# Gathering rows of x for the first two pairs of each loop before the projected tables are stored

## What is computed

```
h = max(layernorm(x), 0);  xl = h@Wl+bl;  xr = h@Wr+br
m = leaky_relu(xl[src] + xr[dst] + w1*We);  logits = m@att
alpha = softmax of logits over the edges of one dst
x1 = x + batchnorm(gelu(h + sum(xl[src]*alpha) + bias))
h1 = max(layernorm(x1), 0)
e = relu(layernorm([h1[src], h1[dst]] @ msg_w + msg_b)) * w
messages = sum(e over dst) / count
out = x1 + gate*relu(layernorm([h1, messages]@upd_w + upd_b)) + (1-gate)*h1
```

## Time and profile before

| | us |
|---|---|
| median of 3 runs | 2380.59 (2380.45 to 2383.5) |
| the profiled execution | 2381.25 |
| its span in the trace | 2379.4 |
| busy: POOL, PE, DVE, ACT | 1612.2, 1634.4, 1535.0, 1021.9 |

### The profile page before, as it was taken

The page is one execution under the profiler, slowest core; times in us unless marked ns, Lnnn a source line. Parts: engine busy times, 40 slices in busy tenths (PEclk is TensorE's granted clock), DMA queues, the critical chain, the costliest instruction groups (busy, mean ns, idle before and its releaser), DMA issues.

```text
span 2379.4 us, 44459 instructions
## 1 busy us (share of the span) xinstructions
PE 1634.4 (69%) x9871; PEld 1205.1 (51%) x9934; DVE 1535.0 (65%) x4997; ACT 1021.9 (43%) x3829; POOL 1612.2 (68%) x1685
## 2 busy tenths in 40 slices
PE   5377787777777777878477776666766666666653
PEld 4255555555555555555365554444544445445542
DVE  7455656656656555655668766667666666666658
ACT  5143444443434443434443544444444434444337
POOL 1577777777777777777017777777777777777740
PEclk9699889888989999889677888888888888888786
DMA  8544444444444444443433434434344343343432
GB/s 229 145 87 94 93 87 95 89 91 94 91 91 94 86 95 93 88 94 76 130 116 72 102 88 94 92 86 93 85 94 92 86 94 84 94 92 88 92 91 68
DMA packets 208000, 228.63 MB, mean 96 GB/s; under 512 B 103119, under 2 KB 153700, under 8 KB 207877
## 3 DMA queue, kind: packets, MB, share of 16 engines
q0 software_dynamic: 54224, 112.59, 24.1%
q1 hardware_dynamic: 153046, 114.71, 17.4%
q10 hardware_dynamic: 672, 0.69, 0.1%
HBM read 194.60 MB, written 33.24 MB: 96 GB/s over the span
## 4 chain that ended last, share of the span: by engine, by line
POOL 51%; issue 19%; PE 12%; DMA 7%; DVE 6%; ACT 2%; POOLq 1%; SPq 1%; DVEq 0%; ACTq 0%
POOL room L692 51%; DMA room<-src_table,rec 6%; PE psum L800 2%; PE psum L861 2%; PE psum L782 1%; PE psum L725 1%; PE psum L772 1%; PE psum L866 1%; PE psum L767 1%; DVE stats L1220 1%; PE psum L879 1%; PE psum L790 1%; DMA room<-state 1%; ACT node_h L969 1%; PE psum L895 0%
## 5 line engine op out<-in xcount | busy, mean ns | idle before, releaser
L692 POOL DMA_INDIRECT room<-src_table,rec x1664 | 1597.2, 960 | 638.5 <-issue 495.9
L861 PE MATMUL psum<-room,ident 128*128 128x384 f32 (+1 forms) x512 | 298.2, 671 | 352.4 <-DMA room<-src_table,rec 317.8
L1105 ACT ACTIVATE room<-psum 128x128 f32<-128x128 f32 x832 | 219.3, 274 | 562.4 <-DVE room L1604 562.2
L1421 DVE TENSOR_TENSOR room<-psum,room 128x384 f32<-128x384 f32 (+1 forms) x256 | 151.1, 590 | 401.8 <-ACT room L1037 267.3
L1037 ACT ACTIVATE room<-psum 128x384 f32<-128x384 f32 (+1 forms) x256 | 131.6, 514 | 548.7 <-PE psum L772 541.0
L1604 DVE TENSOR_TENSOR room<-psum,msg_g 128x384 f32<-128x384 f32 (+1 forms) x256 | 150.5, 588 | 303.9 <-PE psum L866 300.2
L861 PEld LDWEIGHTS psum<-room,ident 128*128 128x128 f32 x512 | 93.9, 229 | 376.0 <-issue 309.0
L866 PEld LDWEIGHTS psum<-room 125*128 125x128 bf16 x2496 | 201.1, 114 | 149.8 <-issue 129.0
L800 PE MATMUL psum<-room 128*125 128x128 f32 x1664 | 264.5, 301 | 16.8 <-ACT room L1055 11.4
L879 PE MATMUL psum<-room 128*125 128x128 f32 x1664 | 273.4, 309 | 1.8 <-ACT room L1117 1.8
L772 PE MATMUL psum<-ident,room 128*128 128x128 f32 x832 | 150.6, 298 | 148.4 <-DMA room<-src_table,rec 146.7
(11 more groups left out here) (181 smaller groups left out, 2142.2 us busy)
## 6 DMA issues: line engine op xcount, KB each, us to landing
room<-dst_perm SPq DMA_DIRECT2D x128, 406.2 KB
room<-src_table,rec POOLq DMA_INDIRECT x1664
room<-dst_table SPq DMA_DIRECT2D x128, 62.5 KB
src_table<-rows SPq DMA_DIRECT2D x24, 224.0 KB
dst_table<-rows SPq DMA_DIRECT2D x24, 224.0 KB
st_in<-state SPq DMA_DIRECT2D x64, 64.0 KB
state<-st_out SPq DMA_DIRECT2D x64, 64.0 KB
st_in<-state SPq DMA_DIRECT2D x64, 62.5 KB
```

The costliest lines, as they stand in the source:

```text
L692: pool.indirect_dma_start(out=xg[:, u, t * P:(t + 1) * P], out_offset=None, in_=src_table[n][:, :], in_offset=bass.IndirectOffsetOnAxis(ap ...
L861: nc.tensor.matmul(msg_bank[b][:, cols], ident[:, :], xg[:, u, t0 * P:t1 * P], start=True, stop=False, skip_group_check=True)
L1105: i = nc.scalar.activation(sq[:, j * P:(j + 1) * P], msg_bank[b][:, j * P:(j + 1) * P], ACT.Square, accum_out=var_e[:, c, j:j + 1])
```

## The change

Gathers of the first two pairs (`RAW = 2`) of each loop read rows of x itself (loop 1) or of x1 (loop 2, from a new array `x1_rows` that SP stores), so they need no table. The gathered rows are then normed (DVE statistics, ACT scale), transposed (PE), relu (ACT), projected (PE) and the bias added (DVE), in place in `xg`. For pair 0 this stands before loop 1 (`raw_first`) and inside the own phase of the middle; for pair 1 it stands inside slot 0 and the start of slot 1 of each loop (`raw_second`).

The opening is also in another order. The number row of the destinations is loaded first on ACT's queue, ahead of the four arrays of weights, and is turned into float by ACT (it was POOL); POOL permutes it (it was ACT) and stores records and permutation (it was SP); `chunk_spans` on DVE stands before the first bias add, not before the fourth; 14 arrays of weights that only the second half needs are loaded by POOL after loop 1 (they were loaded by SP in the opening), and DVE centres `msg_w` there. SP loads the destinations of the first two pairs behind the last table rows, not ahead of them.

```diff
+RAW = 2
+            gather_pair(0, gat, 0, 0)
...
+            gather_pair(0, gat, 1, 1)
...
+            tables_stored(0)
+            def first_slot(k, u, end):
+                if type(k) is not int or k >= RAW:
+                    gather_pair(0, gat, k, u)
+            all_pairs(pool, first_slot, last, 0)
+            for to, v in last_weights:
+                pool.dma_start(to, v).then_inc(s_wc, 16)
...
+            for g, (t0, t1) in enumerate(GROUPS):
+                sp.wait_ge(s_x1, g + 1)
+                for p0, p1 in NODE_ROWS:
+                    sp.dma_start(node_cols(x1_rows, p0, p1, t0, t1), node_x[p0:p1, t0:t1, :]).then_inc(s_x1_out, 16)
...
+        RAW_NORM, RAW_TURN, RAW_FEATURES, RAW_PROJECT, RAW_ROWS = (range(i, i + 2 * NB, 2) for i in (1, 3, 4, 5, 6))
...
+        def raw_second(pe, n, k, b, weights):
+            if type(k) is int and k == 0:
+                raw_turn(pe, n, 1, b)
+                if b > 0:
+                    raw_project(pe, n, 1, b - 1, weights)
+            if type(k) is int and k == 1 and b == 0:
+                raw_project(pe, n, 1, NB - 1, weights)
...
                 for b in range(NB):
                     if there(k, 0, end):
                         msg_message(k, u, b)
+                    raw_second(pe, 1, k, b, msg_wc)
                     lagged(msg_sums, k, u, b, 3, end)
...
+            act.wait_ge(s_padded, 1)
+            load_field(act, 1)
             for to, v in first_weights:
                 act.dma_start(to, v).then_inc(s_wa, 16)
-            act.wait_ge(s_padded, 1)
-            load_field(act, 1)
+            act.wait_ge(s_padrow, 3)
+            act.wait_ge(s_edges[1], 48)
+            nc.scalar.activation(dst_f[0:NCH + 1, :], raw[0:NCH + 1, 1, :], ACT.Copy).then_inc(s_dstf, 1)
...
+            def raw_norm(n, r, b):
+                act.wait_ge(s_norm_scale, raw_part(n, r) + 1)
+                for t in range(*BLK[b]):
+                    rows_t = xg[:, r, t * P:(t + 1) * P]
+                    i = nc.scalar.activation(rows_t, rows_t, ACT.Identity, bias=raw_nmr[:, r, t:t + 1], scale=raw_rstd[:, r, t:t + 1])
+                i.then_inc(s_norm, 1)
...
-            tables(1, msg_b, {})
+            tables(1, msg_b, {11: lambda: raw_scale(1, 0, msg)})
+            raw_scale(1, 1, msg)
```

More of the change, by code:

```diff
@@ L445, in _ @@
             sp.wait_ge(s_padded, 1)
[L446 removed]
+            for f in (0, 2, 3):
                 load_field(sp, f)
@@ L560, in first_records, with first_destinations @@
             def first_records(n, s):
-                for k in range(3):
+                for k in range(RAW if n == 0 else 0, 3):
                     load_rec(s, k, k)
+            def first_destinations(n, s):
                 firsts = []
@@ L664, in _, with gather_pair @@
             pool.wait_ge(s_padrow, 3)
-            n = NCH + 1
-            pool.wait_ge(s_edges[1], 48)
-            pool.tensor_copy(dst_f[0:n, :], raw[0:n, 1, :]).then_inc(s_dstf, 1)
+            def gather_pair(n, s, k, u):
+                pool.wait_ge(s.rec[u], turns(s, k, u, U, 16, last))
+                first_rows = type(k) is int and k < RAW
+                table = (a["x"], x1_rows)[n] if first_rows else src_table[n]
+                for b, (t0, t1) in enumerate(BLK):
+                    if type(k) is not int or k >= U:
+                        if n == 0:
+                            pool.wait_ge(s.sum, nth(k - U, b + 1))
+                        else:
+                            pool.wait_ge(s.m, nth(k - U, b + 1))
+                    settle(pool)
+                    for t in range(t0, t1):
+                        pool.indirect_dma_start(
+                            out=xg[:, u, t * P:(t + 1) * P], out_offset=None, in_=table[:, :],
+                            in_offset=bass.IndirectOffsetOnAxis(ap=rec[:, u, t:t + 1].bitcast(I32), axis=0),
+                        ).then_inc(s.xg[u][b], 16)
@@ new lines, in tables_stored @@
+            def tables_stored(n):
+                for u in range(3):
+                    pool.wait_ge(s_src_out[u], 32 * (n + 1) * SLOT_GROUPS[u])
+            last = 0
+            gather_pair(0, gat, 0, 0)
+            pool.wait_ge(s_dstf, 1)
+            settle(pool)
+            for c0, c1 in STORE_ROWS:
+                pool.dma_start(rec_rows[c0:c1, 1, :], dst_f[c0:c1, :]).then_inc(s_rec, 16)
+            pool.wait_ge(s_edges[0], 48)
+            settle(pool)
+            for c0, c1 in STORE_ROWS:
+                pool.dma_start(rec_rows[c0:c1, 0, :].bitcast(I32), raw[c0:c1, 0, :]).then_inc(s_rec, 16)
@@ L1346, in list_block @@
                 dve.drain().then_inc(s_blk3, 1)
-            tables(0, b_lr, {0: opening, 1: lambda: x_stats(3), 2: later_columns, 3: chunk_spans, 6: count_pairs,
-                             7: lambda: list_block(0)})
-            edge_row_parts()
-            rest_of_weights(0)
+            last = 0
+            tables(0, b_lr, {0: opening, 1: lambda: x_stats(2), 2: lambda: x_stats(3), 3: later_columns, 6: count_pairs,
+                             7: lambda: list_block(0), 9: edge_row_parts, 11: lambda: rest_of_weights(0)})
+            raw_scale(0, 0, gat)
             rest_of_weights(1)
@@ L1512, in batch_stats @@
                 i.then_inc(s_bnst, 1)
+            dve.wait_ge(s_wc, NWC * 16)
+            dve.tensor_reduce(wmean[:, 0:2], msg_w[:, :, :], AX_X, ALU.add)
+            link(dve.tensor_reduce(wmean[:, 2:3], msg_b[:, D:2 * D], AX_X, ALU.add))
+            link(dve.tensor_scalar(wmean[:, 0:3], wmean[:, 0:3], 1.0 / D, None, ALU.mult))
+            for h in range(2):
+                link(dve.tensor_scalar(msg_wc[:, h * D:(h + 1) * D], msg_w[:, h, :], wmean[:, h:h + 1], None, ALU.subtract))
+            link(dve.tensor_scalar(msg_b[:, D:2 * D], msg_b[:, D:2 * D], wmean[:, 2:3], None, ALU.subtract))
+            dve.drain().then_inc(s_centred, 1)
             done = 0
```

265 lines of the change are left out of this document (183 added, 82 removed).

## The result

The changed kernel takes 2398.22 us (median of 6 runs, 2391.51 to 2401.17), the kernel before 2380.88 (6 runs, 2379.04 to 2383.5): ratio 1.0068, 95% interval 1.0055 to 1.0082. It is slower by 17 us. The prediction was 2372 with a range to 2388. The profiled execution took 2400.21 us, with a span of 2398.4.

What follows compares the result with a forecast made beforehand. It took the starts of late gathers, gated by ring and records, to bound the kernel. From 2381.25 us: loop 1 -21, middle +1, loop 2 +11, together -9, giving 2372; range 2357 to 2388.

Steps and rivals of the forecast that it cites:

- What bounds the kernel: Both loops: a loop ends as late as its gathers were started, so starts of late gathers are compared, 16.3 us a pair.
- The opening: Before loop 1: last add at about 65, POOL starts pair 2 10 us earlier, PE starts loop 1 at 90 as now.
- I take the first add at 24.3: Opening, DVE's first bias add: moved from 19.96 to 24.3, chunk work covered by a 4.13 us wait and 2.02 us of statistics.
- From the first add to the end of the last: Opening's tables: 2.0 us statistics, 3.0 weights' remainder, 1 smaller piece added, 5.9 removed, 2 us stall; last add at about 65.
- Slot 0 of loop 1: First slot, blocks one after another: 23 us in place of 12.0; pair 4 gathered at 123, 21 us gained (10 to 28).
- Middle and own phase: Between the loops: 1 us lost to weights (0 to 3), own phase starting at 1247, 2.5 us more inside it (0 to 7).
- Loop 2: Slot 0 takes 29 us (27 to 34), slot 1 17; pair 5 gathered at 1337, 11 us lost (3 to 22).
- Clock in the own phase: PE between the loops: low clock kept, granted 0.53; 13 transposes and projections take 10 us, against 5 at full clock.
- The second table load: ACT's second function table: counted with 1.28 us; with the skill page's drain of 1.38 us the sum would be 2373.4.
- B: Rival: PE stays at the low clock, own phase 6.5 us more, loop 2 loses 22, loop 1 gains 12; 2392, chance 0.17.
- D: Rival: opening or pair 0's raw chain 7 us late, gain 14 against loss 12 and 1; 2380, chance 0.15.
- A: Rival: slots keep up and POOL runs on, both loops give their 26 gathers; at most 2311, put at 2340, chance 0.07.

Runs made afterwards that it cites:

- features_late: Changed kernel with checked loop counts, ScalarE's features(g) again behind deviations and norm_rows(g + 2) in opening and middle; ratio 1.0062.
- copy_late: Changed kernel with weights first, features late, chunk work at group 3, pair 1's record behind group 2's stores, ScalarE's destinations copy behind features(1); 2382.70 us.
- one_raw_loop1: copy_late with only pair 0 raw in loop 1 and no raw pairs in loop 2; 2356.44 us.
- stats_early: copy_late with pair 0's statistics and scale moved from behind the tables into them, at group 5; 2385.60 us.
- opening_again: copy_late with ScalarE's copy of the destinations back at the head of its work; 2389.21 us.
- weights_second: copy_late with the weights issued behind the destinations again; 2389.31 us.
- weights_features: Changed kernel with weights first and features late, destinations copy and chunk work left as in the change; 2390.28 us.
- the control: Changed kernel with two loop counts checked against their bounds when loaded, run on the slower chip; 3108.95 us, ratio 1.0079.

## Why the prediction was wrong, point by point

- **What bounds the kernel** held: the marks at which late gathers start carried every total in the table, and the loops behind them kept their pace.
- **The opening failed**, and with slot 0 it took the whole gain of loop 1. Pair 4 was to be gathered at 123 and came at 148.25: 18.7 of these 25 us stand at PE's start of loop 1 (108.67 against 90), 5 in slot 0, 2 between the sum and the gather. The failed step is "I take the first add at 24.3", which rested on the 4.13 us wait and 2.02 us of statistics as a cover. It measured 37.02. All three pieces were named in that step, the copy, the second table and the features ahead of the square root "that wait for weights which now come second", and none was followed to a time. The copy put the first square root from 9.26 to 16.35. The weights, issued 2.6 us later than before, landed at 26.08, 21.2 us after their issue instead of 9.0; the sum had given this place, with the copy and the table load, 4.3 us in all. The chunk work, taken as 5.9 us, was to be hidden by the wait ahead of the first add. The wait stood ahead of it instead, for the second square root; it came at 28.33, took 8.5 us and lay bare. In features_late it did not: it began at 20.5, and the first add still waited 4.34 us for PE behind it. By the runs the copy and the weights are worth 9 us each with all else restored, and the order of the features 5 to 8 behind them. With the opening restored the time is that of the kernel before (2382.70), so this step explains the loss, but not all of the distance to the forecast.
- **From the first add to the end of the last** I took 41 us; 44.9 were measured, and 42.7 in copy_late. From there to the start of loop 1: taken 25, measured 27 and 26. The stall of 2 us on ScalarE's part was 7.8 at group 4 in the changed kernel (the add at 57.79 waits for PE), 0.5 in copy_late. That PE starts at 90.00 with the opening restored, where I had it at 90, is in part luck: the first add came 3 us earlier than in the forecast, the rest took 3 longer.
- **Slot 0 of loop 1**: taken 23, measured 28.0 and in copy_late 27.4. I took 5.5 to 6.7 us a block; blocks 1 to 3 took 7.2 to 7.8. One link was missing: the transposes of block 2 of pair 1 wait for VectorE to have emptied their bank, 3.60 us in the row at 126.22. Slot 1 to its sum: taken 10, measured 9.6. So even with the opening restored the gain was 16 (copy_late), not 21.
- **Middle and own phase**: weights 1 us, measured none (they are centred at 1148.15, under the wait for the state). The own phase was to start 9.3 us later, and starts at 1254.78, 17.1 later, of which 5.3 to 6.5 come from loop 1: 11 to 12 where 9.3 were taken.
- **Loop 2** held: slot 0 taken 29 (27 to 34), measured 32.4; slot 1 taken 17, measured 15.4; the loss of middle and loop 2 taken as 12, measured 13.9 in the distance. In copy_late it was 17.9, in the other kernels with two raw pairs 14 to 17: where loop 1 ends earlier, the loss of loop 2 is not smaller.
- **Clock in the own phase.** I let it stay at the 1.2 GHz level, with a granted clock of 0.53 before. It did not. The stretch now:

```profile
core 0: us, PE busy (x) PEld busy (x) DVE busy (x) ACT busy (x) POOL busy (x), PEclk, DMA share, GB/s
1255.00:1285.00 30.00, 18.01 (x123) 16.16 (x123) 28.44 (x53) 9.54 (x29) 23.60 (x22) 0.89 0.19 49
```

Eight update matmuls take 1.12 us from 1262 on, behind the first transposes of raw rows, instead of 2.06. In one_raw_loop1, without raw work there, they take 2.06 again. It brought no time, since VectorE is busy for 28.44 of 30 us. The Trainium skill (TensorE: Matmul & The Clock Gate, Part 1) says that activity releases the throttle; this trace agrees, with 0.89 granted where 0.53 was.

- **The second table load.** The rows at 12.15 and 15.05 are each followed by their operation 1.30 us after their start. The Trainium skill (ScalarE: Activation LUTs, What ACT_TABLE_LOAD costs) counts a further drain of 1.38 us; no row here shows one.
- **The rivals.** B named a slower end (2392) by the low clock in the own phase; the time came near it, the mechanism did not. D, an opening "7 us late", had the right place and too small a size (18.7 at PE's start of loop 1). A assumed that the slots keep up. With one raw pair in each loop they do, and the gain is 35 us (2348.68 against 2383.39 on the same chip).

What stays open: why loop 2's distance is 4 us longer in copy_late than in the changed kernel. Four more kernels with copy_late's code behind loop 1 (stats_early, opening_again, weights_second, weights_features) have 215.3 to 218.3, so the features' order in the middle does not settle it. Open too is what the chunk work's place costs without the two gates.

## What to carry to other kernels

When a change moves a load or an operation to the head of an in-order queue, follow every wait behind it to a time, and do not take the landing of a load from its issue: the last weights were issued 2.6 us later and landed 15 later, while the destinations, moved from second place to first, landed 3 to 4 earlier. Two gates side by side hide each other: mending one showed 1 to 6 us of 16 here, so test with all restored and put back one at a time. Work that brings a pipeline's first item forward is worth having for the first item alone; the second's, put in the serial start of the loop, cost here more than the gathers it saved (2365 to 2356 us without it in loop 1; loop 2 lost 13 us with two and gained 8 with one).

## What the hardware showed that I had not expected

- Loads of 4 weight tensors, issued 2.6 us later than before and behind the destinations, held PE until 24.7 to 26.1 us in all eight kernels that have them so; issued first, they never did (13.13 in copy_late, released by ScalarE). The last of them took 21.2 us from issue to landing instead of 9.0.
- A VectorE operation of 0.15 us took up to 2.82 us when it stood beside POOL's cast of 65 x 1664 numbers, and ended with it, in six kernels.
- On one chip every kernel took 1.3 times as long (3085.99 us for the kernel before) with the same durations of instructions (a gather in the middle of loop 1 took 952 ns there and 956 in the changed kernel here). What grew were waits, in the control POOL's for records above all:

```profile
POOL room L690 <- DMA rec<-rec_rows: 347.5, 49, 28.2
POOL room L690 <- remote: 171.8, 81, 2.4
```

In the changed kernel on its own chip the records held it for 40.6 us in 4 waits. Why the waits were longer on the other chip was not looked into. The ratio to the kernel before was the same within its interval.
